# Norm and all projections of a batch moved into one front stage, with their results passed through DRAM

## The reference, cut to what matters

```
x = x + ga * attn(layernorm(x) * (1 + ca) + sa)          # 4 batches, 2048 tokens, 512 channels
    attn: q, k, v = split(h @ Wqkv.T + bqkv)              # 16 heads of 32
          q, k = rope(q), rope(k);  y = softmax(causal(q k^T / sqrt(32))) v;  y @ Wo.T + bo
x = x + gb * moe(layernorm(x) * (1 + cb) + sb)            # top 8 of 48 kept experts, capacity 192
```

## Time and profile before

| | us |
|---|---|
| measured, median of 3 (lowest, highest) | 4920.65 (4919.97, 4927.16) |
| profiled execution, its own time | 4923.3 |
| its span, first to last instruction | 4921.5 |
| PE busy in the span | 4400.7 (89%) |
| DVE, ACT, POOL busy | 2712.7, 2240.2, 1632.7 |
| mean granted TensorE clock | 0.934 |
| start of a batch to start of the next | 1094.3, 1092.3, 1092.2 |

### The profile page before, as it was taken

One profiled execution on the slowest core, in us unless ns is written; L12 is line 12 of the kernel. 1 busy time (PEld: TensorE's weight loads), 2 busy tenths in 40 slices (PEclk: granted clock), 3 DMA queues, 4 the chain that ended last, 5 costly groups with the idle time before them and its releaser, 6 DMA issues.

```text
span 4921.5 us, 75676 instructions
## 1 busy us (share of the span) xinstructions
PE 4400.7 (89%) x19552; PEld 2341.7 (48%) x19552; DVE 2712.7 (55%) x5795; ACT 2240.2 (46%) x4226; POOL 1632.7 (33%) x1079
## 2 busy tenths in 40 slices
PE   4899999985899999885999999875999999877998
PEld 2445454344445444353445444353545444356776
DVE  2546556564546546474555646464554646475565
ACT  1356556721355657521355657531465657421111
POOL 1142534311142534312152434302153443303554
PEclk7899999986899999997899999987899999978999
DMA  3111112122111112122112112122121212128998
GB/s 126 44 35 49 49 44 61 57 87 78 48 38 49 50 33 70 48 93 78 41 40 50 49 31 70 58 92 73 37 57 36 54 34 72 59 79 222 257 258 199
DMA packets 185430, 369.47 MB, mean 75 GB/s; under 512 B 44340, under 2 KB 47540, under 8 KB 183348
## 3 DMA queue, kind: packets, MB, share of 16 engines
q1 hardware_dynamic: 163512, 306.26, 21.9%
q0 software_dynamic: 21504, 58.40, 5.1%
HBM read 195.48 MB, written 84.68 MB: 57 GB/s over the span
## 4 chain that ended last, share of the span: by engine, by line
PE 75%; issue 11%; DVE 5%; ACT 4%; DMA 2%; POOL 1%; POOLq 1%; ACTq 1%; SPq 0%; DVEq 0%
PE PS L1070 22%; PE PS L1032 14%; PE PS L1052 10%; PE PS L1015 9%; PE PS L1172 5%; PE PS L1023 5%; PE PS L1183 3%; PE PS L1098 2%; ACT Pt L901 2%; PE PS L1055 1%; DMA xin<-x 1%; PE PS L1111 1%; DVE stA L1252 1%; PE PS L1158 1%; PE PS L1143 1%
## 5 line engine op out<-in xcount | busy, mean ns | idle before, releaser
L901 ACT ACTIVATE Pt<-PS 128x512 f32<-128x512 f32 (+3 forms) x2560 | 1230.2, 534 | 936.5 <-PE PS L1055 476.8
L1316 DVE TENSOR_REDUCE part<-PS 128x1 f32<-128x512 f32 x1536 | 1021.3, 686 | 968.4 <-PE PS L1032 966.0
L1070 PE MATMUL PS<-Pt,V 128*64 128x512 f32 (+3 forms) x5120 | 1280.3, 561 | 0.0
L1052 PE MATMUL PS<-QK 97*128 97x512 f32 (+3 forms) x2560 | 880.1, 409 | 62.4 <-ACT Pt L901 43.0
L1032 PE MATMUL PS<-QK 96*128 96x512 f32 (+3 forms) x2560 | 891.3, 431 | 32.1 <-DVE part L1316 17.8
L791 POOL TENSOR_TENSOR ot<-ot,od 32x512 f32<-32x512 f32 x256 | 325.6, 1272 | 1626.5 <-ACT od L887 1620.8
L1032 PEld LDWEIGHTS PS<-QK 96*128 96x128 f32 x2560 | 403.3, 195 | 876.3 <-DVE part L1312 350.1
L1312 DVE CUSTOM_DVE_ANT_0 PS<-PS,consts 128x384 f32<-128x384 f32 (+3 forms) x1024 | 500.8, 495 | 244.1 <-PE PS L1032 242.4
L1052 PEld LDWEIGHTS PS<-QK 97*128 97x128 f32 x2560 | 482.1, 194 | 248.5 <-ACT Pt L901 102.4
L1015 PE MATMUL PS<-hT,W 128*128 128x512 f32 x1024 | 465.8, 600 | 14.0 <-ACTq L528 14.0
L1070 PEld LDWEIGHTS PS<-Pt,V 128*64 128x64 f32 x5120 | 256.1, 135 | 311.5 <-issue 249.9
(11 more groups left out here) (152 smaller groups left out, 4273.5 us busy)
## 6 DMA issues: line engine op xcount, KB each, us to landing
QK<-st SPq DMA_DIRECT2D x768, 128.0 KB, 2.4
Wg<-wgu SPq DMA_DIRECT2D x48, 768.0 KB
Wd<-wdn SPq DMA_DIRECT2D x48, 384.0 KB
xin<-x SPq DMA_DIRECT2D x16, 1024.0 KB, 6.2
table<-modd SPq DMA_DIRECT2D x64, 256.0 KB, 4.0
xc<-x SPq DMA_DIRECT2D x16, 1024.0 KB, 7.6
out<-x SPq DMA_DIRECT2D x16, 1024.0 KB, 4.3
table<-h SPq DMA_DIRECT2D x16, 1024.0 KB, 6.3
```

The source lines that it names most:

```text
L901: nc.scalar.activation(Pt[:, t % NPT, first:CH], S2[t % NS2][:, first:CH], ACT.Exp, scale=SCALE).then_inc(exp_done, 1)
L1052: last = mm(S2[t % NS2][:, first:CH], QK[0:3 * HD + 1, hh % 2, 1, k * P:(k + 1) * P], QK[0:3 * HD + 1, hh % 2, 0, j * CH + first:(j + 1) * ...
L1070: last = mm(O[j % 2][2 * i * HD:2 * (i + 1) * HD, first:CH], values_and_ones(g, kb + i, hh % GH), Pt[:, (2 * n + i) % NPT, first:CH], star ...
L1316: v.reduce_max(part[:, qb, cc:cc + 1], s1[:, 0:w], AX.X).then_inc(s1_dve, 1)
```

## The change

- The norm stage is no longer a stage of its own. Two `meet`s per batch are left of three.
- A new list `front()` replaces `opening()`. It walks all 16 chunks n = 4 j + g (token chunk j outer, group g inner): two `proj`, `shuffle`, `mul` twice (the former `turn`), `high` and `split` of chunk n-1, one `vproj` and what `spread[n]` holds, then `sum`. `vproj(j, t)` now takes 128 tokens against all 512 value channels (4 matmuls, 8 records of 128x512) instead of four token tiles against one group's 128. All of `sum` and `split` is on DVE.
- `spread` holds the norm of the next token chunk (`stat`, then four `turn`s, now the transposes) and the max tiles of head 0 for its first three query chunks, four or three at a place, so that 16 are left for `stream()`, four to a unit.
- The front stage has five PSUM banks `FB` of its own (those of scores and values); `qraw`, `qs`, `t1`, `st` have two buffers; `hT` holds two token chunks and not the batch. The norm is done in place in `xin`. The transposes of a chunk start when all four of its tiles are normed.
- `W` of all groups, `cos` and `sin` are loaded once ahead of the batch loop. `W` is loaded in pieces of 512 bytes.
- Every chunk of q and k parts is stored whole (1 MB) to `qkd` in DRAM; heads 1 to 15 stack from there, head 0 from `st`. Values are stored to `vd` (1 MB per token chunk) and, for group 0, copied into `V` by DMA in pieces of 128 and 256 bytes; groups 1 to 3 are loaded from `vd`, once a group, during the second head of the group ahead.
- After chunk 15 SP waits for all these stores before it stacks head 1.
- `stream()` has no projections. The first token chunk of a batch is loaded ahead of the `meet`, the second just after it.

```diff
+def front():
+    spread[3] = tiles(0)
+    spread[6], spread[7] = tiles(1)[:4], tiles(1)[4:]
+    spread[8] = [("most", 0, 0), ("row", 0, 0), ("negated", 0, 0)]
+    for i, step in enumerate(tiles(2)):
+        spread[10 + i // 3].append(step)
+    for j in range(NCH - 1):
+        spread[NG * j].append(("stat", j + 1))
+        for ct in range(KT):
+            spread[NG * j + 1 + ct // 2].append(("turn", j + 1, ct))
+    out = [("stat", 0)] + [("turn", 0, ct) for ct in range(KT)]
+    for n in range(NCK):
+        j, g = divmod(n, NG)
+        out += [("proj", n, 0), ("proj", n, 1), ("shuffle", n), ("mul", n, 0), ("mul", n, 1)]
+        if n:
+            out += [("high", n - 1), ("split", n - 1)]
+        out += [("vproj", j, g)] + spread[n] + [("sum", n)]
+    return out + [("high", NCK - 1), ("split", NCK - 1)]
...
-    for i in range(FIRST_HALF, NTILE):
-        beside[(i - FIRST_HALF) // 6].append(("max", 0, i))
+    for i in range(LAST_CHUNK, NTILE):
+        beside[(i - LAST_CHUNK) // 4].append(("max", 0, i))
...
-    for g in range(1, NG):
-        at = NU * GH * (g - 1)
-        for j in range(NCH):
-            beside[at + VALUES_FROM + VALUES_EVERY * j].append(("vproj", g, j))
-            n = at + TURN_FROM + TURN_EVERY * j
-            beside[n].append(("proj", g, j, 0))
...
+                def store_parts(n):
+
+                    j, g = divmod(n, NG)
+                    wait_apart(sp, q_lo, NCK * b + n + 1)
+                    if g == 0:
+                        stack(0, j, st[0:HD, n % 2].bitcast(F32))
+                    sp.dma_start(qkd[b, g, :, :, j * CH:(j + 1) * CH], st[:, n % 2].bitcast(F32)).then_inc(st_out[n % 2], 16)
...
+                for n in range(NCK):
+                    j, g = divmod(n, NG)
...
+                    if g == 0 and j > 0:
+                        store_values(j - 1)
+                    store_parts(n)
+                store_values(NCH - 1)
+                for i in range(2):
+
+                    wait_apart(sp, st_out[i], 16 * (NCK // 2) * (b + 1))
+                    wait_apart(sp, v_out[i], 64 * (NCH // 2) * (b + 1))
                 for hh in range(1, H + 1):
...
-                            stack(hh, j)
+                            stack(hh, j, qkd[b, g, h * HD:(h + 1) * HD, :, j * CH:(j + 1) * CH])
...
+                    if h == 1 and g + 1 < NG:
+                        load_values(g + 1)
...
+                        _, j, t = step
+                        for k in range(KT):
+                            last = mm(bank, hT[:, j % 2, k, t * P:(t + 1) * P], W[:, k, 2], start=k == 0, stop=k == KT - 1)
+                        last.then_inc(valued, 1)
```

More of the change, by code:

```diff
@@ L103, in extent @@
     return first, (r + 1) * P - first if k >= TPC * j else 0
[L106 to L112, removed]
+def front():
     def tiles(j):
         return [("max", 0, i) for i in range(NTILE) if TILES[i][0] // TPC == j]
-    return (rotated(0) + split(0) + rotated(1) + split(1) + rotated(2) + split(2) + rotated(3) + tiles(0) + split(3)
-            + tiles(1) + [("most", 0, 0), ("row", 0, 0), ("negated", 0, 0)])
+    spread = [[] for _ in range(NCK)]
+    spread[3] = tiles(0)
[15 more added lines that the diff above has]
+    return out + [("high", NCK - 1), ("split", NCK - 1)]
 FIRST_HALF = sum(qb < NT // 2 for qb, _, _ in TILES)
-TILES_FROM, VALUES_FROM, VALUES_EVERY, TURN_FROM, TURN_EVERY = 2, 6, 8, 2 * NU - 4, 5
+LAST_CHUNK = sum(qb < NT - TPC for qb, _, _ in TILES)
+TILES_FROM = 2
 def stream():
@@ L164, in stream @@
     for n in range(NU * H):
[L165 to L166 removed]
+        out.append(("score", *divmod(n, NU)))
         if n >= 2:
             out.append(("value", *divmod(n - 2, NU)))
[L169 removed]
+        out += beside[n] + closing[n]
     for n in range(NU * H, NU * H + 16):
@@ L174, in stream, with taken_by @@
     return out
[L177 to L186, removed]
+NV, NPT_B = NU * H, 2 * NU * H
+STEPS = front() + stream()
+USES = [step for step in STEPS if step[0] in ("max", "row")]
+EMPTIED = {step: n + 1 for n, step in enumerate(step for step in STEPS if step[0] in ("max", "vproj"))}
+FIRST = [step for step in STEPS if step[0] in ("turn", "proj", "vproj")]
+N_USE, N_ROW, N_DVE, N_FIRST, N_V = len(USES), 2 * H, len(EMPTIED), len(FIRST), NT
+N_QT = N_FIRST - N_V
+NFB = 5
+def taken_by(step):
+    return [use for use in FIRST if use[0] != "vproj"].index(step) + 1
 def routing():
@@ L398, in adaln_block @@
         O = [PS[:, 6], PS[:, 7]]
+        FB = [PS[:, 3 + i] for i in range(NFB)]
         ident = K[:, K_ID:K_ID + P]
@@ L559, in _ @@
             wait_apart(sp, mod_out, 80)
-            with sp.Fori(0, NB) as b:
[L562 to L581, removed]
@@ new lines, in _ @@
+                    if kind == "turn":
+                        _, j, ct = step
+                        pe.wait_ge(xhat_ready, ONE + TPC * (NCH * b + j + 1))
+                        for t in range(TPC):
+                            last = nc.tensor.transpose(bank[:, t * P:(t + 1) * P], xin[j % 2][:, t, ct * P:(ct + 1) * P], ident)
+                        last.then_inc(turned, 1)
+                    elif kind == "proj":
+                        _, n, i = step
+                        j, g = divmod(n, NG)
+                        if n == 0 and i == 0:
+                            pe.wait_ge(w_in, ONE + 176)
+                        if g == 0 and i == 0:
+                            pe.wait_ge(f_act, ONE + N_QT * b + taken_by(("turn", j, KT - 1)))
@@ L1244, in _ @@
             with dve.Fori(0, NB) as b:
-                meet(dve, 3 * b + 1)
-                with dve.Fori(0, NCH // 2) as jj:
-                    for u in range(2):
-                        ci = NCH * b + 2 * jj + u
+                meet(dve, 2 * b + 1)
+                v.tensor_copy(modb[:, :], modc[:, b, :]).then_inc(modb_set, 1)
+                swap = list(range(HD // 2, HD)) + list(range(HD // 2))
+                n0, n1 = 0, 0
+                for step in STEPS:
+                    kind = step[0]
+                    if kind == "stat":
+                        j = step[1]
+                        ci = NCH * b + j
+                        own = xin[j % 2]
                         a.begin(ci)
-                        dve.wait_ge(x_in[u], ONE + 32 * b + 16 * jj + 16)
+                        dve.wait_ge(x_in[j % 2], ONE + 32 * b + 16 * (j // 2) + 16)
                         for t in range(TPC):
-                            last = v.bn_stats(stA[:, t, :], xin[:, u, t, :])
+                            last = v.bn_stats(stA[:, t, :], own[:, t, :])
                         a.link(last, passed)
```

392 lines of the change are left out of this document (195 added, 197 removed).

## The result

The changed kernel takes 4749.65 us (median of 4 runs, 4746.46 to 4752.76) against 4920.31 for the kernel before on the same chip (4 runs, 4918.82 to 4927.16): a ratio of 0.9652, with a 95% interval of 0.9637 to 0.9667. The forecast was 4791 with a range of 4715 to 4880. The profiled execution of the changed kernel has a span of 4744.3 us and a mean clock of 0.950; before it was 4921.5 and 0.934.

The account below looks back on a forecast made before the run. The prediction took PE to bound the heads. Heads save 131.7 us a batch, start to end of head 0 adds 95.5: 36 less a batch, 22 in the first, 130 in all, from 4920.65 to 4791 us, range 4715 to 4880.

Parts of the forecast that it names:

- first projection to V: Front stage, up to V, the end of PE's last value record: set by PE's records, transposes and tiles, 184.3 us.
- V to head 1's first tile: Hand-over after the last value record: stores land, then head 1's stack is issued and lands, 20 us, PE standing for 15.
- the rest of head 0: From head 1's first tile to the end of head 0: 39.4 us of work left plus 9 for low clock.
- Head 0 in all is a plain head and 16 tiles: Head 0's work: 40.4 us as in a head without projections, plus 4 for tiles, 44.4 us.
- DVE too is late: At the hand-over, head 0's tiles stand behind the last chunk's `split` on DVE; no separate size given.
- the rival of a slow front: Front stage set by a chain through ACT, POOL and DVE; at 2 us more a chunk, 4919 us; 8%.
- the first eight records at half clock cost 3 more: Start of the front stage: PE's first eight records run at half clock, adding 3 us.
- 10.8 or less in mean: Sign in the profile: front stage chunks with tiles and transposes take at most 10.8 us in mean; 12 means bound elsewhere.
- Every head waits for its stack: Stack landing from DRAM delays each head's first tile; free to 4.9 us, then 60 us per us; 4921 and up; 7%.
- The hand-over is hidden: Before head 1: stores land almost at once and the clock does not fall, 14 + 9 us a batch back, 4699; 12%.
- the clock comes back at once: After the hand-over: PE is full from head 1's first tile and the clock recovers as at 108, 4767 us; 10%.
- The clock stays low through head 0: After the hand-over: half clock lasts through head 0, 12 us more a batch, 4839 us; 15%.

Follow-up runs that it names:

- stack_late2: The changed kernel with two spare 1 MB stores issued ahead of each stack of heads 2 to 11: 4929.1 us, ratio 1.0016 to the kernel before.
- after: The changed kernel itself, as measured and profiled, against the kernel before: 4749.65 us, ratio 0.9652.
- last: h1_order with weights and tables loaded early, memsets unmoved, and chunk 14's `split` moved with chunk 15's last steps: 4696.97 us, ratio 0.9547 to the kernel before.
- h1_from_st: The changed kernel with head 1 stacked from `st` beside head 0, SP waiting for the stores only before head 2: 4732.22 us, ratio 0.9609.
- h1_order: h1_from_st with chunk 15's `sum`, `high` and `split` moved behind head 0's tiles of the second unit: 4714.56 us, ratio 0.9577 to the kernel before.
- start2: The changed kernel with weights and tables loaded right behind the constants, POOL's memsets behind chunk 0's second rope product: 4743.77 us, ratio 0.9645.
- start: The changed kernel with weights and tables loaded right behind the constants, POOL's memsets behind the first inverse root: 4745.16 us, ratio 0.9639.

## Why the prediction was right, and what it had wrong

The direction and the mechanism held: projections out of the heads, a front stage set by PE, one new stall with a low clock at the hand-over. It was 41 us too high. In spans it had 130 of the 177 us; the missing 47 divide as follows. A minus is time that the forecast had too much.

| term | forecast | measured | over the batches |
|---|---|---|---|
| heads 1 to 11 | 444.4 | 445.3 | +4 |
| start to first projection, later batches | 13.7 | 13.1 | -2 |
| the same, first batch | 32 | 34.7 | +3 |
| first projection to V | 184.3 | 182.0 (184.2 in the third) | -7 |
| V to head 1's first tile | 20 | 21.4 | +6 |
| the rest of head 0 | 39.4 + 9 | 39.8 | -34 |
| end of head 11 to the next batch | 343.6, as before | 340.1 | -13 |

Each term is read in the first batch (the later start in the second) and taken times the batches it holds for, those of the front stage and of the last row batch by batch. The rows add up to 43. Another 2 us are the kernel before's: it took 172.2 and 172.0 us to the end of head 0 in its third and fourth batch, where the sum went by 170.9. The rest is rounding.

**The term that was mis-sized is "the rest of head 0", 48.4 us for 39.8.** The mechanism was right, the size not. "Head 0 in all is a plain head and 16 tiles" counted 40.4 us from last score to last score, of which 5 were to be done before the stack landed. But in the plain head of before the first tile of the next head comes 6.9 us after that mark (822.64 in the earlier trace rows against 815.75 in the earlier trace rows). From the tile on 33.5 us are left, and with one more for four tiles 34.5, not 39.4. That is 4.9 us of double counting. The clock is the other part: it was low for 11.2 us from the tile on (303.18 to about 314.4), so it cost 5.6 us and not 9. Together that is 40.1 us where 39.8 were measured. The Trainium skill, "TensorE: Matmul & The Clock Gate", section "Part 1: The HAM clock gate", has activity release the throttle, and the prediction had 3 us by it; this case lies between the 3 and the 9.

My evidence against that rule was read too narrowly. Half clock lasted from 161.0 to 208.8 us in the kernel before, 48 us and not 42, and PE was not full in it. Windows of PE in the kernel before, on both sides of the one at 192 to 198 in the earlier trace rows:

```profile
162.00:168.00 6.00, 2.27 (x5) 0.50 0.27 63
...
198.00:204.00 6.00, 4.15 (x12) 0.50 0.29 94
```

How soon the clock comes back is not the same each time, and no run here tells what decides it. From the end of the last longer wait it took 4.6 us in stack_late2 (442.89 to 447.5), 11.2 in after, and 13.3 in last (275.26 to 288.6), with PE busy for almost all of each.

**The hand-over** came out at 21.4 us for 20, by partly other steps. I put 15 us of PE standing down to the DMAs. In the trace its waits are 1.48 and 4.15 us on DVE and 5.77 on the DMA, and between them PE works at half clock. h1_from_st shows that the DMA's part is worth 4.4 us a batch, and h1_order that DVE's order is worth another 4.4. "DVE too is late" stood in the prediction and was given no price.

**The front stage** was PE's, with PE 96.8% busy at clock 1.00: the rival of a slow front is out. Its mean is 182.0 / 16 = 11.4 us a chunk. The 2.3 us that it had less than forecast are a term that mostly did not occur: "the first eight records at half clock cost 3 more". In the first, second and fourth batch the clock was at 1.00 before the first projection (at 99.4 in the first); in the third it came 4.4 us after it, and there the stage took 184.2. The line "10.8 or less in mean" did not follow from the prediction's own sum, which gives 184.3 / 16 = 11.5.

**Rivals.** *Every head waits for its stack* does not happen: the landing from DRAM is 3.0 us, heads 1 to 11 take 40.5 each. The room that the prediction worked out was right in kind: 1 MB more is free, 2 MB cost 179.5 us and turn the whole change into no gain. The price of 60 us for each microsecond left out the clock, 65 of those 179.5. *The hand-over is hidden* and *the clock comes back at once* did not come true either; last comes near the number of the first of them, 4699, but 18 us of it are the early weights, and its clock still falls. *The clock stays low through head 0* is out by the windows 312 to 324. The slow side of the late stack was given as 4970 at a landing of 8 us; by its own 60 us for each microsecond over 4.9 it is 4791 + 186 = 4977.

**Open.** The time between the end of head 11 and the next batch, in code that is the same: 340.1, 337.2 and 342.5 us in after's first three batches, where the kernel before has 343.6, 345.1 and 344.0, and in the last batch no difference to the end of the program. Among the variants it goes from 336 to 344 us, from batch to batch of one execution too. So it is mostly scatter of that stage, and 13 of the 47 us are not the change's by anything shown.

## What to carry to other kernels

A stage that is moved out of a PE-bound loop is worth its PE time only if the new stage feeds PE without a gap: here the interleaving of the norm alone carried 135 of the 171 us. Read PE's busy time together with its clock: here more of the saved busy time was clock than work. Price a hand-over from the first instruction that waits to the next fixed mark, taken from the same two points in a plain round, or work is counted twice. On an in-order engine, work that PE does not need yet belongs behind the reads that free PE's banks, or into a time when PE is busy with something else: `split` moved from under a value projection to behind it cost about 20 us a batch. When one wait was removed here, the next one took the clock down: 1.5 and 0.4 us close together in h1_order, 4 us in last. So look for the last gap before counting on the clock.

## What the runs showed of the hardware

**POOL's memset holds DVE.** In start2 the copy of 16 columns at 65.33 takes 0.18 us; in after at 1128.67 it takes 3.27 us and ends within 0.1 us of the memset's end. Four tiles of the norm take 6.90 us beside the memsets and 1.92 without. The Trainium skill, "SBUF — State Buffer", section "Who interferes with whom", makes the ports that the two share an exclusive lock for copies and tensor_scalar in their fast mode; these two rows agree.

**Two-input products slow each other.** In the front stage of after, groups of instructions (mean ns of one):

```profile
L787 POOL TENSOR_TENSOR qs<-qs,cs 128x1024 f32<-128x1024 f32 x16 | 52.5, 3280 | 0.0
...
L1329 DVE TENSOR_TENSOR st<-t,st 128x1024 fp32r<-128x1024 f32 x15 | 31.7, 2116 | 0.0
```

Before, where they did not overlap, POOL's second product (L748, of the same form) took 2.36 us in the mean of four and `split` 1.22. Both are about 0.9 us longer, so not only the later one pays.

**SP is held by tiny DMAs.** The load of `bqg`, 8 bytes a partition, behind a piece of `W` keeps SP for 2.3 to 2.5 us three times out of four, and in start, where it comes right behind the constants, the first one for 15.1 us; an issue of other loads there takes 0.4 to 0.7. SP's timeline of after:

```profile
66.53 2.49 SPq L569 DMA_DIRECT2D bqg<-bqk  x1
```
